# Loading the second attention's first group and the output stage's first operands in earlier stages, in a two-layer transformer kernel on one core

## The chip, the cores and the metric

The kernel runs on one core of one Trainium2 chip. The metric is the device time of one execution in microseconds (us). Three runs of the kernel before gave 3108.98, 3108.89 and 3117.94 us, median 3108.98. A time is told as a difference to that median.

## The reference

The program computes two recurrent layers over x of shape (2, 2048, 256), each of the form `x = x + s * silu(f)` on a layer-normed input. In the first layer `s` is a linear attention and `f` a small transformer block with a mixture of experts. The second layer, with which this change deals, is

```
xn = layernorm(x)
q, k, v = xn @ Wq, xn @ Wk, xn @ Wv            # 16 heads of 32 (real and imaginary halves of 16)
p = softmax(causal(q . k / 4))                 # over 2048 positions
s = concat_heads(p @ v) @ Wo                   # 512 -> 256
f = xn @ quantised_kernel + bias + (xn @ a) @ b
out = x + s * silu(f)
```

All matrix products of the last two stages but the scores are in float32.

## The kernel before, in words

The kernel is a sequence of stages written with hand-placed semaphores. Each stage is a block in which the five engines run their own instruction streams, and a stage ends with a barrier of all engines. The last three stages are these.

**combine_and_project** (tag `p2`) ends the first layer and computes q, k, v and f of the second for eight blocks of 512 rows. Blocks 0 to 3 are the first sequence, 4 to 7 the second. For each block TensorE makes q and k (`L2751`), v (`L2759`) and f (`L2769`), ScalarE writes the upper float16 halves of q and k into `parts` (`L2554`), VectorE the lower halves (`L2651`), and SyncE (SP) stores them in DRAM with four transfers of 512 KB (`L2502`) and v with four of 256 KB (`L2506`). Before ScalarE overwrites `parts` in block b it waits until all stores of block b-1 have landed (`part_out`), and before it overwrites `vt` it waits for the v stores (`v_kept`). SP's queue in a block is: the load of x for block b+2 (`L2485`), the q stores, the k stores, the v stores.

**wide_attention** (tag `at1`) handles 8 groups of 4 heads: groups 0 to 3 are the first sequence. Tiles QT, KT and V of a group are double buffered by `g % 2`, and a group is loaded by six transfers of 512 KB for QT and KT (each of three row bands of 32 holds an upper or a lower half) and one of 1 MB for V, all issued by SP. Work is cut in units (g, u): u is a block of 512 queries. The order of all instructions is fixed beforehand by a small planner, `wide_schedule`, which gives one list `body`; every engine walks that list. Its events are

- S: a score tile in query-major form, only to find row maxima (PE `L990`, VectorE `L932` and `L938`). There are three slots, so S runs at VectorE's pace.
- M, T: the maxima of a unit are turned into a strip of 8 rows of shifts, and SP copies them into rows 96 and 97 of QT with four transfers of 2 KB (`L838`). These are called the strip transfers.
- ST: a score tile in key-major form, with the shifts as two more rows of the contraction (PE `L998`), then the exponential (ScalarE `L912`). The first ST of a unit waits for the unit's strip transfers (`row_ready`).
- PV, SM, A, N, EV: product with V, row sums and output of the unit, which SP stores into `att` (`L824`, 256 KB).

PE runs its instructions in the order of the list, so an S tile that stands behind an ST in the list waits with it. Near the start the list is: 20 S, of which 16 are the unit (0, 0), with M among them, then T of (0, 0), eight S, and the first ST.

In the kernel before, group 0 is loaded at the start of this stage in three portions: columns 0 to 511 of QT by SP and of KT by ScalarE's queue, then the four shift rows of KT, columns 512 to 1023, and a quarter of V. The rest follows behind the strip transfers of unit (0, 0), and group 1 behind those of unit (0, 1). Group g + 2 is loaded when the last unit of group g has ended.

**finish** (tag `fi`) computes `out = x + att @ Wo * g` for 32 tiles of 128 rows. SP loads a 1 MB tile of `att` for each block of 512 rows (`L2793`, `L2799`) and Wo (`L2794`, 512 KB). Each tile is four float32 products of 128 by 256 on PE (`L2841`), a multiplication (`L2824`) and an addition (`L2827`) on VectorE. ScalarE's queue stores blocks of four tiles, 512 KB each (`L2805`). PE, VectorE and ScalarE run hardware loops over blocks.

Of the kernel before, what the change touches and what calls it, by code (L numbers as in the profile page):

```python
# [5 lines left out]
F32 = mybir.dt.float32  # L6
F16 = mybir.dt.float16
# [6 lines left out]
P = 128  # L14
B, T, D, H = 2, 2048, 256, 16
GROUPS = 8
HG = 4
# [705 lines left out]
def wide_attention(nc, tag, C, q_hi, q_lo, k_hi, k_lo, v, out):  # L723
# [17 lines left out]
    with Ctx(nc, tag) as c:  # L741
        QT = [c.sb(f"qT{k}", [P, HG, T], F16) for k in range(2)]
        KT = [c.sb(f"kT{k}", [P, HG, T], F16) for k in range(2)]
        V = [c.sb(f"v{k}", [P, NKC, HG * 32], F32) for k in range(2)]
# [8 lines left out]
        turned = c.sb("turned", [P, QB // 32, 32], F32)  # L753
        column = c.sb("column", [P, QB // 32], F32)
        share = c.sb("share", [P, QB // 32, 32], F32)
# [8 lines left out]
        first_ld = c.sem("first_ld")  # L764
        early_ld = c.sem("early_ld")
        first_v = c.sem("first_v")
        const_ld = [c.sem(f"const_ld{k}") for k in range(2)]
# [23 lines left out]
        def load_qk(eng, g, cols, sem, only=(0, 1)):  # L791
            k = g % 2
            for dst, src, r, which in ((QT, q_hi, 0, 0), (KT, k_hi, 0, 1), (QT, q_lo, 1, 0), (KT, k_hi, 1, 1),
                                       (QT, q_hi, 2, 0), (KT, k_lo, 2, 1)):
                if which not in only:
                    continue
                eng.dma_start(dst[k][r * hd:(r + 1) * hd, :, cols],
                              src[g].rearrange("h d t -> d h t")[:, :, cols]).then_inc(sem, 16)

        def load_v(eng, g):  # L800
            eng.dma_start(V[g % 2][:, :, :], v[g]).then_inc(v_ld[g % 2], 16)

        def load(eng, g):
            load_qk(eng, g, slice(0, T), qk_ld[g % 2])
            load_v(eng, g)

        @block.sync
        def _(sp):
            load_qk(sp, 0, slice(0, QB), first_ld, (0,))
            def shift_rows(k):  # L810
                for h in range(HG):
                    sp.dma_start(KT[k][K:K + 2, h, :], C["shift_rows"][2 * h:2 * h + 2, h, :]
                                 ).then_inc(const_ld[k], 16)

            shift_rows(0)
            load_qk(sp, 0, slice(QB, 2 * QB), early_ld)
            sp.dma_start(V[0][:, 0:4, :], v[0][:, 0:4, :]).then_inc(first_v, 16)
            ended = []

            def store(unit):  # L820
                g, u = unit
                t = place_of[unit]
                sp.wait_ge(scaled, t + 1)
                sp.dma_start(out[g, :, u * QB:(u + 1) * QB], otile[:, t % 2, :]).then_inc(out_stored[t % 2], 16)  # L824

            for ev in body:
# [6 lines left out]
                if ev[0] == "T":  # L833
                    g, u = ev[1]
                    w = place_of[ev[1]]
                    sp.wait_ge(strip_ready, w + 1)
                    for h in range(HG):
                        sp.dma_start(QT[g % 2][K:K + 2, h, u * QB:(u + 1) * QB],  # L838
                                     strip[2 * h:2 * h + 2, w % 2, :]).then_inc(row_ready[w % 2], 16)
                    if w == 0:  # L840
                        sp.dma_start(V[0][:, 4:NKC, :], v[0][:, 4:NKC, :]).then_inc(v_ld[0], 16)
                        load_qk(sp, 0, slice(2 * QB, T), qk_ld[0])
                    elif w == 1:
                        shift_rows(1)
                        load(sp, 1)
                elif ev[0] == "EV" and ev[1] == last_unit[ev[1][0]] and ev[1][0] + 2 < GROUPS:
                    sp.wait_ge(pv_done, quads_done[ev[1]])
                    load(sp, ev[1][0] + 2)
# [36 lines left out]
        def _(act):  # L885
            load_qk(act, 0, slice(0, QB), first_ld, (1,))
# [96 lines left out]
        def _(pe):  # L983
# [22 lines left out]
            pe.wait_ge(C["const_ready"], C["const_count"])  # L1006
            n = pairs = quads = totals = 0
            loaded, valued, first = set(), set(), False
            for ev in body:
                g = ev[1][0]  # L1010
                if ev[0] == "S":
                    if ev[1] == units[0]:
                        if not first:
                            pe.wait_ge(first_ld, QK_LOADS)
                        first = True
                    elif ev[1] == units[1]:
                        pe.wait_ge(early_ld, QK_LOADS)
                    elif g not in loaded:
                        loaded.add(g)
                        pe.wait_ge(qk_ld[g % 2], QK_LOADS * (g // 2 + 1))  # L1020
# [14 lines left out]
                elif ev[0] == "ST":  # L1035
                    _, (g, u), kc, h = ev
                    if kc == 0 and h == 0:
                        if place_of[ev[1]] == 0:
                            pe.wait_ge(const_ld[0], HG * 16)
                        elif g == 1:  # L1040
                            pe.wait_ge(const_ld[1], HG * 16)
# [5 lines left out]
                elif ev[0] == "PV":  # L1047
# [4 lines left out]
                    if ev[1] == units[0]:  # L1052
                        pe.wait_ge(first_v, 16)
                    elif g not in valued:
                        valued.add(g)
                        pe.wait_ge(v_ld[g % 2], 16 * (g // 2 + 1))
# [60 lines left out]


class Steps:

    def __init__(self, sem, names, credit=2):
        self.sem, self.names, self.credit, self.at = sem, list(names), credit, 0
        assert len(set(self.names)) == len(self.names)

    def start(self, eng, blocks_before=None):  # L1130
        eng.nop().then_inc(self.sem, (self.credit if blocks_before is None else blocks_before)
                           * len(self.names))

    def step(self, name, ins):
        assert self.names[self.at] == name, (self.names[self.at], name)
        self.at = (self.at + 1) % len(self.names)
        return ins.then_inc(self.sem, 1)

    def skip(self, eng, names, blk):

        eng.wait_ge(self.sem, (blk + self.credit) * len(self.names) + self.names.index(names[0]))
        for name in names:
            self.step(name, eng.nop())

    def wait(self, eng, name, blk):

        n = len(self.names)
        eng.wait_ge(self.sem, (blk + self.credit) * n + self.names.index(name) + 1)


def blocks(eng, body, per=2):

    with eng.Fori(0, NB // per) as i:
        for k in range(per):
            body(i * per + k, k, i)


def blocks_ahead(eng, body):

    with eng.Fori(0, NB // 2 - 1) as i:  # L1160
        for k in range(2):
            body(i * 2 + k, k, i, False)
    for k in range(2):
        body(NB - 2 + k, k, NB // 2 - 1, k == 1)


class Banks:


    def __init__(self, c, jobs, steps, ring=8):  # L1170
        assert len(jobs) % ring == 0
        self.jobs, self.steps, self.ring = jobs, steps, ring
        self.index = {j[0]: n for n, j in enumerate(jobs)}
        self.banks = [c.ps(f"bank{k}", [P, QB]) for k in range(ring)]

    def bank(self, name):
        return self.banks[self.index[name] % self.ring]

    def take(self, pe, name, blk, *needs):


        n = self.index[name]
        _, eng, drained = self.jobs[n - self.ring]
        last = {}
        for e, step, ago in needs + ((eng, drained, 0 if n >= self.ring else 1),):
            at = (-ago, self.steps[e].names.index(step), step)
            last[e] = max(last.get(e, at), at)
        for e, (ago, _, step) in last.items():
            self.steps[e].wait(pe, step, blk + ago)
        return self.banks[n % self.ring]  # L1190
# [1183 lines left out]
def combine_and_project(nc, C, W, x, exp_out, gather_at, gate, x_all, mix, kvd, w_out, scale_qk, qk_out, v_out,  # L2374
                        w_saved, w_kept):
# [71 lines left out]
    with Ctx(nc, "p2", reuse=True) as c:  # L2447
# [16 lines left out]
        nT = c.sb("nT", [P, 2, 2, NF, P], F32)  # L2464
# [16 lines left out]
        def _(sp):  # L2481
# [292 lines left out]
def finish(nc, W, att, x_all, g_all, out):  # L2774

    jobs = [(f"x{t}", "dve", f"mul{t}") for t in range(4)]
    dve_names = [f"{s}{t}" for t in range(4) for s in ("mul", "add")]
    with Ctx(nc, "fi") as c:
        w = c.sb("w", [P, 4, D], F32)
        a = [c.sb(f"a{k}", [P, 4, QB], F32) for k in range(NB // B)]  # L2780
        o = [c.sb(f"o{k}", [P, 4, D], F32) for k in range(2)]
        w_ld = c.sem("w_ld")
        ld = [c.sem(f"ld{k}") for k in range(NB // B)]
        stored = [c.sem(f"stored{k}") for k in range(2)]
        pe_s = Steps(c.sem("pe"), [j[0] for j in jobs], credit=NB // B)
        dve_s = Steps(c.sem("dve"), dve_names)
        banks = Banks(c, jobs, {"dve": dve_s}, ring=4)
# [161 lines left out]
```

## Time and profile before

| what | us |
|---|---|
| median of three runs | 3108.98 |
| the profiled execution, its own time | 3104.42 |
| span of the profiled execution, first to last instruction | 3102.5 |
| last instruction of the projection (ScalarE, `L2589`) ends | 1971.2 |
| first instruction on PE in the attention | 1978.9 |
| last store of the attention issued | 3030.2 |
| finish, first load issued to the end of the span | 3032.7 to 3102.5 |

All times on the trace are us from the start of the span, durations too unless a unit is given. A name such as SPq is the queue of an engine: the issue of a transfer, not its movement. "to landing" is the time from issue to the moment when all its data is there. A bracket at the end of a row is the time for which the engine was idle before it, and what ended that.

### The profile page before, as it was taken

The page shows a single profiled execution, that of the slowest core. Times are in us where ns is not written, and L with a number is a line of the kernel's source. Part 1 is how long each engine was busy: PE and PEld are TensorE (multiplying, and loading weights), DVE is VectorE, ACT ScalarE, POOL GpSimd, SP SyncE. Part 2 cuts the span into 40 slices and gives each one's busy share as a digit, 9 for nine tenths or more (in the row PEclk, how much of TensorE's full clock was granted, in tenths as well). Part 3 has the DMA queues.
Part 4 walks back from the last instruction along what each step waited for, and adds up shares of the span by engine and source line. Part 5 has one row for each costly group of instructions (what it writes and reads, how often), then busy time and mean ns, then how long its engine had stood idle before and what let it go on. Part 6 is the DMA issues. An engine that isn't in the chain of part 4 may idle for free. (4 is left out here: it accounts for less than half of the span.)

```text
span 3102.5 us, 46462 instructions
## 1 busy us (share of the span) xinstructions
PE 2850.2 (92%) x18025; PEld 1325.8 (43%) x18025; DVE 2022.6 (65%) x4462; ACT 1520.9 (49%) x2473; POOL 929.4 (30%) x420
## 2 busy tenths in 40 slices
PE   7897999999999963999998799799999999999987
PEld 4664233333333341676666555333333333333326
DVE  6886899999999555000001655588887877878823
ACT  3432577677677741222221444245565665565560
POOL 0001000000000022110001320166777777777780
PEclk9998799999999986999999999899999999999998
DMA  3223222022220034222112344421120220211005
GB/s 123 79 61 90 45 42 46 12 45 49 46 46 12 12 112 117 68 72 85 61 48 80 96 149 144 114 62 39 31 62 12 66 62 8 63 35 42 8 10 174
DMA packets 143625, 196.08 MB, mean 63 GB/s; under 512 B 14000, under 2 KB 109056, under 8 KB 141472
## 3 DMA queue, kind: packets, MB, share of 16 engines
q1 hardware_dynamic: 130304, 170.77, 19.8%
q0 software_dynamic: 6144, 16.79, 2.2%
q10 hardware_dynamic: 6960, 5.58, 0.6%
q8 instruction: 141, 2.31, 0.3%
q14 instruction: 76, 0.62, 0.1%
HBM read 116.81 MB, written 75.76 MB: 62 GB/s over the span
## 5 line engine op out<-in xcount | busy, mean ns | idle before, releaser
L912 ACT ACTIVATE at_probs<-at_st 128x512 f32<-128x512 f32 (+3 forms) x1280 | 588.3, 541 | 444.6 <-PE at_st L998 284.1
L874 POOL TENSOR_TENSOR at_probs<-at_probs 128x2048 f32<-128x2048 f32 (+3 forms) x208 | 732.9, 3528 | 220.6 <-ACT at_probs L912 136.8
L383 DVE TENSOR_REDUCE at_part<-at_s 128x1 f32<-128x512 f32 (+3 forms) x1280 | 689.2, 602 | 67.9 <-PE at_s L421 29.8
L365 ACT ACTIVATE at_probs<-at_st 128x1024 f32<-128x1024 f32 (+3 forms) x640 | 541.6, 895 | 275.9 <-PE at_st L440 138.1
L938 DVE TENSOR_REDUCE at_part<-at_s 128x1 f32<-128x512 f32 x768 | 498.4, 683 | 68.6 <-PE at_s L990 64.6
L990 PE MATMUL at_s<-at_kT,at_qT 96*128 96x512 f16 (+3 forms) x1280 | 391.4, 361 | 28.5 <-DMA at_kT<-klo 10.1
L998 PE MATMUL at_st<-at_qT,at_kT 98*128 98x512 f16 (+3 forms) x1280 | 379.3, 356 | 15.1 <-ACT at_probs L912 10.5
L421 PE MATMUL at_s<-at_kT,at_qT 48*128 48x512 f16 (+3 forms) x1280 | 359.6, 366 | 26.4 <-DMA at_qT<-qhi 10.2
L932 DVE CUSTOM_DVE_ANT_0 at_s<-at_s,at_later 128x384 f32<-128x384 f32 (+3 forms) x512 | 246.8, 497 | 109.4 <-PE at_s L990 109.0
L507 PE MATMUL at_acc<-at_probs,at_v 128*32 128x512 f32 (+3 forms) x2560 | 304.5, 549 | 8.9 <-ACT at_otile L352 8.8
L2319 DVE TENSOR_TENSOR ex_ot<-ex_bank,lin_b 128x512 f32<-128x512 f32 x32 | 22.1, 692 | 437.8 <-PE ex_bank L2349 437.8
L1059 PE MATMUL at_acc<-at_probs,at_v 128*32 128x512 f32 (+3 forms) x2560 | 288.3, 538 | 6.7 <-ACT at_otile L894 6.5
L440 PE MATMUL at_st<-at_qT,at_kT 50*128 50x512 f16 (+3 forms) x1280 | 282.4, 356 | 4.9 <-ACT at_probs L365 3.3
L1886 POOL TENSOR_TENSOR ag_a<-ag_a,ag_r 128x1024 f32<-128x1024 f32 x8 | 18.8, 2359 | 849.3 <-ACT ag_r L1903 849.3
L990 PEld LDWEIGHTS at_s<-at_kT,at_qT 96*128 96x128 f16 x1280 | 109.9, 98 | 355.1 <-DVE at_part L938 153.9
L421 PEld LDWEIGHTS at_s<-at_kT,at_qT 48*128 48x128 f16 x1280 | 100.2, 94 | 369.9 <-DVE at_part L383 318.0
L2292 ACT ACTIVATE ex_hT<-ex_bank,ex_b 128x512 f32<-128x512 f32 x128 | 88.0, 687 | 333.2 <-PE ex_bank L2339 333.2
L2339 PE MATMUL ex_bank<-ex_xT,lin_w 128*128 128x512 f32 x512 | 224.0, 595 | 1.0 <-ACT ex_xT L2285 1.0
L2349 PE MATMUL ex_bank<-lin_w,ex_hT 128*128 128x256 f32 x1024 | 223.7, 379 | 0.8 <-ACT ex_hT L2292 0.8
L2349 PEld LDWEIGHTS ex_bank<-lin_w,ex_hT 128*128 128x128 f32 x1024 | 193.9, 190 | 31.1 <-issue 3.8
L998 PEld LDWEIGHTS at_st<-at_qT,at_kT 98*128 98x128 f16 x1280 | 122.9, 98 | 186.1 <-ACT at_probs L912 106.9
L2034 POOL DMA_INDIRECT lin_xin<-z_rows,lin_rows_at x64 | 60.9, 951 | 297.3 <-PE ex_bank L2330 211.4
(322 smaller groups left out, 3229.9 us busy)
## 6 DMA issues: line engine op xcount, KB each, us to landing
att<-at_otile SPq DMA_DIRECT2D x64, 256.0 KB, 2.1
lin_w<-in_W SPq DMA_DIRECT2D x16, 1024.0 KB, 7.7
at_v<-v SPq DMA_DIRECT2D x14, 1024.0 KB, 14.4
v<-pr_vt SPq DMA_DIRECT2D x32, 256.0 KB, 3.2
exp_out<-ex_ot SPq DMA_DIRECT2D x32, 256.0 KB, 2.1
v<-p_vt SPq DMA_DIRECT2D x32, 256.0 KB, 3.7
fi_a<-att SPq DMA_DIRECT2D x8, 1024.0 KB, 6.0
at_qT<-qhi SPq DMA_DIRECT2D x14, 512.0 KB, 9.3
```

The source lines that it names most:

```text
L365: act.activation(probs[:, quad % RING, heads_down * p:heads_down * (p + 1), off:QB], st_ps[n % st_slots][:, :, off:QB], ACT.Exp, scale=EXP ...
L383: dve.tensor_reduce(part[:, w % 2, qt * HG + h, j:j + 1], s_ps[n % S_SLOTS][:, 0:width], AX.X, ALU.max).then_inc(item_free, 1)
L421: mm = pe.matmul(place[:, 0:width], QT[g % 2][rows, h // heads_down, q0:q0 + P], KT[g % 2][rows, h // heads_down, j * QB:j * QB + width], ...
L440: mm = pe.matmul(place[:, y, off:QB], KT[g % 2][rows, h // heads_down, kc * P:(kc + 1) * P], QT[g % 2][rows, h // heads_down, u * QB + off ...
L507: mm = pe.matmul(acc_ps[32 * h:32 * h + 32, off:QB], V[g % 2][:, kc, 32 * h:32 * h + 32], probs[:, quads % RING, h, off:QB], start=kc == 0 ...
L874: pool.tensor_tensor(total, total, probs[:, slots.slot[quad], :, off:QB], ALU.add).then_inc(add_done, 1)
L912: act.activation(probs[:, slots.slot[quad], h, off:QB], st_ps[n % ST_SLOTS][:, off:QB], ACT.Exp, scale=EXP_SCALE).then_inc(exp_done, 1)
L938: dve.tensor_reduce(part[:, w % 2, qt * HG + h, j:j + 1], s_ps[n % S_SLOTS][:, 0:width], AX.X, ALU.max).then_inc(item_free, 1)
L990: pe.matmul(place[:, 0:width], QT[g % 2][0:K, h, q0:q0 + P], KT[g % 2][0:K, h, j * QB:j * QB + width], start=True, stop=True).then_inc(ite ...
L998: mm = pe.matmul(place[:, off:QB], KT[g % 2][0:K + 2, h, kc * P:(kc + 1) * P], QT[g % 2][0:K + 2, h, u * QB + off:(u + 1) * QB], start=Tru ...
L1059: mm = pe.matmul(acc_ps[32 * h:32 * h + 32, off:QB], V[g % 2][:, kc, 32 * h:32 * h + 32], probs[:, slots.slot[quads], h, off:QB], start=kc ...
L2349: mm = pe.matmul(d[:, t * D:(t + 1) * D], hT[cb][:, n, (2 * m + t) * P:(2 * m + t + 1) * P], w2[e % 2][:, n, :], start=n == 0, stop=n == N ...
```

## The change

- An object `Carried` holds one QT, KT and V tile, which live from the projection to the end, and its semaphores. They serve as buffer 0 of the attention. Group 0 is loaded into them whole by SP, in `combine_and_project` at the start of block 4's turn, with 11 transfers (six of 512 KB, four shift rows of 8 KB, V of 1 MB), after a wait for all stores of blocks 0 to 3. The stage's tile `nT` is laid into the V tile.
- At its start the attention has SP load group 1 (six of 512 KB and V of 1 MB) and then its shift rows. PE waits once for group 0. The portioned loads, and those that ScalarE's queue issued, are gone.
- When the last unit of group 6 has ended, SP waits for the stores issued so far, then loads Wo into the V tile and `att` of blocks 0 to 3 into the QT and KT tiles (`load_finish`, 4.5 MB), ahead of the strip transfers of unit (7, 2).
- `finish` starts with these tiles. It is written out without loops, works on pairs of tiles (128 x 512 on VectorE, six PSUM buffers in place of four) and stores 256 KB at a time.

```diff
+class Carried:
+    def __init__(self, c):
+        self.q, self.k = (c.sb(n, [P, HG, T], F16) for n in ("q", "k"))
+        self.v = c.sb("v", [P, NKC, HG * 32], F32)
+        self.group_ld, self.w_ld = c.sem("group_ld"), c.sem("w_ld")
+        self.a_ld = [c.sem(f"a_ld{k}") for k in range(NB // B)]
+        self.w = self.v[:, 0:8, :].rearrange("p (g c) n -> p g (c n)", g=4)
+        self.a = [t[:, 2 * y:2 * y + 2, :].bitcast(F32).rearrange("p a (b n) -> p (a b) n", n=QB)
+                  for t in (self.q, self.k) for y in range(2)]
+    def load_group(self, eng, C, qk, v):
+        K = 32
+        for dst, src, r in ((self.q, qk[0][0], 0), (self.k, qk[1][0], 0), (self.q, qk[0][1], 1),
+                            (self.k, qk[1][0], 1), (self.q, qk[0][0], 2), (self.k, qk[1][1], 2)):
+            eng.dma_start(dst[r * K:(r + 1) * K, :, :], src[0].rearrange("h d t -> d h t")).then_inc(self.group_ld, 16)
+        for h in range(HG):
+            eng.dma_start(self.k[3 * K:3 * K + 2, h, :], C["shift_rows"][2 * h:2 * h + 2, h, :]
+                          ).then_inc(self.group_ld, 16)
+        eng.dma_start(self.v[:, :, :], v[0, 0]).then_inc(self.group_ld, 16)
+    def load_finish(self, eng, W, att):
+        eng.dma_start(self.w, W["Wo"].rearrange("(g p) n -> p g n", p=P)).then_inc(self.w_ld, 16)
+        for blk in range(NB // B):
+            self.load_value(eng, att, blk)
...
 wide_attention, SP
-            load_qk(sp, 0, slice(0, QB), first_ld, (0,))
...
+            load(sp, 1)
+            for h in range(HG):
+                sp.dma_start(KT[1][K:K + 2, h, :], C["shift_rows"][2 * h:2 * h + 2, h, :]).then_inc(const_ld, 16)
...
-                    if w == 0:
-                        sp.dma_start(V[0][:, 4:NKC, :], v[0][:, 4:NKC, :]).then_inc(v_ld[0], 16)
-                        load_qk(sp, 0, slice(2 * QB, T), qk_ld[0])
-                    elif w == 1:
-                        shift_rows(1)
-                        load(sp, 1)
...
+                    elif g + 2 == GROUPS:
+                        sp.wait_ge(pv_done, quads_done[ev[1]])
+                        for k in range(2):
+                            sp.wait_ge(out_stored[k], issued[k])
+                        carried.load_finish(sp, W, out)
...
 wide_attention, PE
+            pe.wait_ge(carried.group_ld, Carried.GROUP_LOADS)
...
 combine_and_project, SP
                 if b + 2 < NB:
                     load_x(b + 2)
+                if b == NQB:
+                    sp.wait_ge(part_out, 64 * NQB)
+                    sp.wait_ge(v_kept, 64 * NQB)
+                    carried.load_group(sp, C, qk_out, v_out)
...
 finish
+            for n in range(PAIRS):
+                tile, rows = o[:, n % 4, :, :], slice(2 * n, 2 * n + 2)
+                if n >= 4:
+                    dve.wait_ge(stored[n % 4], 16 * (n // 4))
+                pe_s.wait(dve, f"x {n}")
+                dve_s.step(f"mul {n}", dve.tensor_tensor(tile, banks.tile(f"x {n}")[:, :, :], g_all[:, rows, :], ALU.mult))
+                dve_s.wait(dve, f"mul {n}")
+                dve_s.step(f"add {n}", dve.tensor_tensor(tile, tile, x_all[:, rows, :], ALU.add))
```

## Rows read from the trace of the kernel before

**Rows 1.** First line of the profile's page.
```profile
span 3102.5 us, 46462 instructions
```
**Rows 2.** Chain that ended last, from 2950 us: start, us, what.
```profile
3032.73 0.37 SPq L2793
...
3033.45 6.48 DMA fi_w<-in_Wo
...
3040.28 57.53 PE fi_bank L2841 x256
...
3098.49 0.43 DVE fi_o L2827
```
**Rows 3.** Line 824 (min/median/max ns, first and last start), and the last output store.
```profile
L824 SPq DMA_DIRECT2D att<-at_otile x32: 320/321/430, 2019.7 to 3030.2; - x32
...
DMA to landing us min/median/max: 2.1/2.1/18.7
...
out<-fi_o ACTq DMA_DIRECT2D x1, 512.0 KB, 2.9
```
**Rows 4.** Stretches of 1 us in finish: us, PE, PEld, DVE, ACT, POOL, clock, DMA share, GB/s.
```profile
3043.00:3044.00 1.00, 1.00 (x4) 0.82 (x3) 0.00 (x0) 0.00 (x0) 0.00 (x0) 0.50 1.06 391
...
3045.00:3046.00 1.00, 1.00 (x6) 0.90 (x5) 0.20 (x1) 0.00 (x0) 0.00 (x0) 1.00 1.04 387
```
**Rows 5.** Timeline of the attention's start: start us, us, engine, line, work, [idle before].
```profile
1972.53 0.33 SPq L797 DMA_DIRECT2D at_qT<-qhi  x1
...
1973.21 0.29 POOL L858 TENSOR_SCALAR_AFFINE_SELECT at_later<-at_later 128x128 bf16<-128x128 bf16 x1
...
1978.95 0.48 PE L990 MATMUL at_s<-at_kT,at_qT 96*128 96x128 f16 x3 [10.08 <-DMA at_kT<-klo]
1979.36 0.30 DVE L932 CUSTOM_DVE_ANT_0 at_s<-at_s,at_later 128x128 f32<-128x128 f32 x1 [6.68 <-PE at_s L990]
...
1989.39 2.45 SPq L838 DMA_DIRECT2D at_qT<-at_strip  x4
...
1993.01 0.59 PE L998 MATMUL at_st<-at_qT,at_kT 98*128 98x512 f16 x1 [0.51 <-DMA at_qT<-at_strip]
```
**Rows 6.** SP's queue at two group loads, and V's time to landing in each.
```profile
2016.18 0.33 SPq L797 DMA_DIRECT2D at_qT<-qhi  x1
...
2019.24 0.43 SPq L801 DMA_DIRECT2D at_v<-v  x1
...
at_v<-v SPq DMA_DIRECT2D x1, 1024.0 KB, 18.5
...
2408.27 0.32 SPq L797 DMA_DIRECT2D at_qT<-qhi  x1
...
2411.91 0.43 SPq L801 DMA_DIRECT2D at_v<-v  x1
...
at_v<-v SPq DMA_DIRECT2D x1, 1024.0 KB, 16.4
```
**Rows 7.** The projection at block 4: SP's queue, two times to landing, ScalarE.
```profile
1868.62 0.87 SPq L2485 DMA_DIRECT2D p_xs<-in_x  x1
1880.56 0.36 SPq L2502 DMA_DIRECT2D qhi<-p_parts  x1
...
1888.82 0.51 SPq L2502 DMA_DIRECT2D klo<-p_parts  x1
...
v<-p_vt SPq DMA_DIRECT2D x1, 256.0 KB, 4.2
...
klo<-p_parts SPq DMA_DIRECT2D x1, 512.0 KB, 4.1
...
1902.52 3.23 ACT L2554 ACTIVATE p_parts<-p_bank,all_score 128x1024 f16<-128x1024 f32 x3
```
**Rows 8.** SP's queue late in the attention: strip transfers of units (7, 2) and (7, 1), (7, 0).
```profile
2917.92 2.40 SPq L838 DMA_DIRECT2D at_qT<-at_strip  x4
...
2959.93 14.04 SPq L838 DMA_DIRECT2D at_qT<-at_strip  x8
```

More of the change, by code:

```diff
@@ L789, in wide_attention, with load @@
         block = c.block()
-        def load_qk(eng, g, cols, sem, only=(0, 1)):
+        def load(eng, g):
             k = g % 2
[L793 to L805, printed above, removed]
+            for dst, src, r in ((QT, q_hi, 0), (KT, k_hi, 0), (QT, q_lo, 1), (KT, k_hi, 1), (QT, q_hi, 2), (KT, k_lo, 2)):
+                eng.dma_start(dst[k][r * hd:(r + 1) * hd, :, :],
+                              src[g].rearrange("h d t -> d h t")).then_inc(qk_ld[k], 16)
+            eng.dma_start(V[k][:, :, :], v[g]).then_inc(v_ld[k], 16)
         @block.sync
         def _(sp):
-            load_qk(sp, 0, slice(0, QB), first_ld, (0,))
[L810 to L818, printed above, removed]
+            load(sp, 1)
+            for h in range(HG):
+                sp.dma_start(KT[1][K:K + 2, h, :], C["shift_rows"][2 * h:2 * h + 2, h, :]).then_inc(const_ld, 16)
+            ended, issued = [], [0, 0]
             def store(unit):
@@ L885, in _ @@
         def _(act):
-            load_qk(act, 0, slice(0, QB), first_ld, (1,))
             n, ended = 0, []
@@ L1116 @@
 EPS = 1e-5
[L1119 to L1190, printed above, removed]
 class Chain:
@@ L2771, in _, with finish @@
                 step(f"y {b}", mm)
-def finish(nc, W, att, x_all, g_all, out):
-    jobs = [(f"x{t}", "dve", f"mul{t}") for t in range(4)]
-    dve_names = [f"{s}{t}" for t in range(4) for s in ("mul", "add")]
+def finish(nc, carried, att, x_all, g_all, out):
+    PAIRS = NT // 2
+    jobs = [(f"x {n}", ("dve", f"mul {n}")) for n in range(PAIRS)]
     with Ctx(nc, "fi") as c:
[L2779 to L2787, printed above, removed]
-        rows = att.rearrange("(b g) r t -> b r g t", b=B)
+        a, w = carried.a, carried.w
+        o = c.sb("o", [P, 4, 2, D], F32)
+        stored = [c.sem(f"stored{k}") for k in range(4)]
+        pe_s = Marks(c.sem("pe"), [j[0] for j in jobs])
+        dve_s = Marks(c.sem("dve"), [f"{s} {n}" for n in range(PAIRS) for s in ("mul", "add")])
+        banks = Banked(c, "bank", [(n, (dve_s, done)) for n, (_, done) in jobs], 6, (P, 2, D))
         block = c.block()
@@ L2801, in _ @@
         @block.scalar
         def _(act):
[L2803 to L2809 removed]
+            rows = out.rearrange("b (n p) d -> p (b n) d", p=P)
+            for n in range(PAIRS):
+                dve_s.wait(act, f"add {n}")
+                act.dma_start(rows[:, 2 * n:2 * n + 2, :], o[:, n % 4, :, :]).then_inc(stored[n % 4], 16)
@@ L2831, in _ @@
         @block.tensor
         def _(pe):
-            pe_s.start(pe)
-            pe.wait_ge(w_ld, 16)
-            def body(blk, k, i):
-                pe.wait_ge(ld[k], i * 16 + 16)
-                for t in range(4):
-                    d = banks.take(pe, f"x{t}", blk)
+            pe.wait_ge(carried.w_ld, 16)
+            for n in range(PAIRS):
+                blk = n // 2
+                k = blk % (NB // B)
+                if n % 2 == 0:
+                    pe.wait_ge(carried.a_ld[k], 16 * (blk // (NB // B) + 1))
+                d = banks.take(pe, f"x {n}")
+                for y in range(2):
+                    t = 2 * (n % 2) + y
```

153 lines of the change are left out of this document (62 added, 91 removed).

## The prediction

> **What bounds the kernel now.** I read the span first [rows 1]: 3102.5 us, against 3104.42 us as the profiled execution's own time, so 1.9 us lie around the trace. The median of the runs shown, 3108.98 us, is 4.6 us above that execution; I work out a difference on the trace and subtract it from the median. The change touches two seams between stages and one stretch in the middle of the projection, so the question at each seam is what ends the idle time there.
>
> At the last seam the chain of waits tells it [rows 2]. SP issues the first load at 3032.73, Wo at 3033.45, Wo is there after 6.48 us, and PE starts at 3040.28. From then on PE alone is the chain, 57.53 us for 32 tiles. Nothing else is on it but the last multiplication, addition and store.
>
> At the seam in front of the attention the timeline tells it [rows 5]. SP's first load goes out at 1972.53, PE had been idle for 10.08 us when it starts at 1978.95, and a transfer ended that. VectorE begins at 1979.36. From there the order is: S tiles at VectorE's pace, the strip transfers issued from 1989.39 to 1991.84, and the first ST at 1993.01, for which PE had waited only 0.51 us. So before, the strip transfers were hardly late.
>
> **Finish: removed wait.** Wo and four blocks of `att` are in place, so PE needs only the barrier. Any instruction behind it can begin when SP's could, at 3032.73; I take 3032.8. That is 3040.28 - 3032.8 = **-7.5 us**, from -7.3 to -7.6. The wait that comes next is the one ahead of it: the last store of the attention, issued at 3030.2 and landed 2.1 us later [rows 3], which the change leaves alone. The first products still run at the low clock: the granted clock is 0.50, the 1.2 GHz level, in the fourth microsecond of PE's work and 1.00 two microseconds later [rows 4]. PE will have been idle for a shorter time before it. Whether its clock is then higher no row shows, so I take nothing for that and put a gain of up to 1.5 us into the bounds, less than the four slow microseconds would give.
>
> **Finish: pairs in place of tiles, no loops.** PE's work is the same. A pair takes PE 57.53 / 16 = 3.6 us. One VectorE instruction on 128 x 256 took 0.43 us [rows 2]; on twice the columns it takes between 0.43 and 0.86, and two of them stay under 1.8 us, hidden behind PE. Only the last pair shows: two instructions longer by about 0.27 each, +0.5 (0 to +0.9). The last store is half as large: 512 KB took 2.9 us to landing and 256 KB took 2.1 on the other queue [rows 3], so -0.8 (-0.8 to 0). Together **-0.3 us**. The loops' own cost doesn't show as a gap on PE; up to -0.5 for it in the range.
>
> **Attention's start: what the engines gain.** PE's first S can start at the barrier, about 1972.6. VectorE's first S needs the mask that GpSimd ends at 1973.21 + 0.29 = 1973.50, so VectorE starts at about 1973.6 instead of 1979.36, 5.8 us earlier. It sets the pace until T, so the strip transfers would be issued from 1983.6 and the first ST start at 1987.2.
>
> **Attention's start: what the queue takes back.** SP now issues 4 MB of group 1 and four shift rows first, from 1972.53, before it comes to the strip transfers. Their issue is over by 1978, so SP itself is free at 1983.6; the question is when the data moves. Two group loads show how long 4 MB take: 2016.18 to 2019.24 + 18.5 = 2037.7, that is 21.6 us, and 2408.27 to 2411.91 + 16.4 = 2428.3, that is 20.0 us [rows 6]. The attention's store issued at 2019.7, right behind the first of these, took 18.7 us to land where the median is 2.1 [rows 3]: it landed at 2038.4, 0.7 us behind V. So a transfer on SP's queue waits for all that was issued before it. By this V of group 1 lands between 1992.5 and 1994.1. The shift rows and strips behind it take some tenths to 1.2 us more (1.2 is what lay between the last strip's issue and the ST before, 1991.84 to 1993.01). The first ST starts at 1993.0 to 1995.3; I take 1994.3. PE meets this ST in its fixed order after eight more S, so from about 1987 on it stands still, and with it VectorE, whose S tiles lie behind the ST. The 5.8 us of lead are lost: from the first ST everything runs as before, but **+1.3 us** late (0 to +2.3). What was moved away (the rest of group 0, group 1) hid behind computing before, and gives nothing.
>
> The Trainium skill, page "DMA: Bandwidth & Descriptors", section "Queues, rings and completion order", says that each DMA engine takes descriptors in ring order but that completion is not in order per issuing engine; the section on why a DMA increments its semaphore by 16 adds that a transfer over two partitions uses only two engines. By that the strips wait for two engines' share and not for the slowest of 16, and the first ST could be 1 or 2 us earlier than 1994.3.
>
> **The projection.** At block 4 SP waits for the v stores of block 3, whose last is issued just before 1868.62 and takes 4.2 us, so until about 1872.3, and issues 11 transfers in 5 us; its next duty is at 1880.56 [rows 7], so the issue is hidden. The x load issued at 1868.62 is ahead in the queue. The 4 MB move until about 1873.5 + 20.6 = 1894.1. The q stores (1880.56) and k stores (until 1888.82) queue behind. 1 MB of them takes at most the 4.1 us of the last one's landing, nearer 3.2 when they stream, so the k stores land at about 1900.9. ScalarE overwrites `parts` at 1902.52. The margin is 1.6 us: **0 us** (0 to +3, if the load or the stores take 4 us more). v and the next x load follow 3 and 5 us later, ahead of their use. If this cover went, PE would stop for want of free banks, one for one.
>
> **Late attention.** `load_finish` stands in front of the strips of unit (7, 2), issued at 2917.92. The 4.5 MB move at the rate of `att` loads, 387 GB/s [rows 4], in 12 us, or at the group loads' rate in 24. The first ST of (7, 2) comes about when the strips of (7, 1) are issued, 2959.93 [rows 8]; there are 42 us of cover, so 0. SP's wait for earlier stores costs at most the 2.1 us of a store's landing, under the same cover.
>
> **The sum**: -7.5 - 0.3 + 1.3 + 0 + 0 = -6.5 us. Against the profiled execution 3104.42 - 6.5 = 3097.9; against the median 3108.98 - 6.5 = **3102.5 us**. A measurement of this kernel can tell about 0.3% (9.3 us) from no change, so this forecast lies within it.
>
> **The rivals.** *The strips are not held back.* Then the start keeps its 5.8 us and the sum is -7.8 - 5.8 = -13.6: 3095.4 us. For it: the strips are 2 KB each, and no row before shows one behind a group load. Against it: the store that took 18.7 us. The Trainium skill's rule above, that completion is not in order per issuing engine, would allow it if the strips' engines ran ahead; ring order on each engine speaks against it. Chance 0.08.
>
> *More is gained than I count.* The mechanism is mine but the strips land 2 us earlier, the clock rises 1.5 us earlier in finish, and the written-out loops give 0.5: -10.5, 3098.5 us. Chance 0.2.
>
> *The projection stalls, and the kernel is slower than before.* Place: ScalarE's wait for block 4's stores ahead of `parts` of block 5. It turns the sign when the k stores land over 1.6 + 6.5 = 8.1 us later than I reckon, after 1909, for instance if the group load took 29 us in place of 20.6 beside a busy PE and VectorE. Each further microsecond costs one, and block 5's x load and v stores are held as well. With a load of 38 us the time is 3112 us, and slower by over 0.3% needs 3118. Against it: the loads of rows 6 ran beside full engines too, and lay between 20.0 and 21.6 us. Chance 0.05 for a loss.
>
> *The change does not do what it says*: group 0 isn't there at the barrier. It is issued 100 us before; no chance of note.
>
> **How the numbers follow.** My forecast has 0.67, the larger gain 0.2, free strips 0.08, a loss 0.05. The forecast's own bounds are 3100 to 3105.5. The range reaches to 3095.5 for the larger gain and most of the free strips, and to 3107.5 for a projection stalled by a few microseconds. Faster by over 0.3% means under 3099.7: all of the free strips, most of the larger gain, and some of the forecast's edge, 0.32. Slower by over 0.3%: 0.03. The rest, 0.65, is within.
>
> **What would show it.** In the profile after: PE's first product in finish directly behind the barrier, some 3 us after the last `att` store; the first S right after 1972.6 and VectorE at 1973.6; the first ST with an idle time of about 7 us ahead, put down to the strip transfer, 21 to 22 us after SP's first load; the projection as long as before; no idle time at the first ST of (7, 2). I am wrong if the first ST starts near 1987, if ScalarE waits in block 5 of the projection, or if the 1040 us between the first ST and the last store change their length by more than 2 us.

## The result, and the profile after

The changed kernel takes **3104.62 us** (median of 20 runs, 3101.92 to 3111.45), the kernel before 3110.87 us in the same session (20 runs, 3106.62 to 3118.58). The ratio is 0.998, with a 95% interval from 0.9973 to 0.9987: 6.2 us less, where 6.5 were forecast.

The profiled execution after took 3104.14 us, its span is the line below. It looks as long as that of before [rows 1], and this is the first trap of the case. The page's first line:

```profile
span 3102.4 us, 46189 instructions
```

The two executions were not equally quick ahead of the change. The x load that SP issues last before block 4's turn stands at 1868.62 us before [rows 7] and at 1874.96 after, though nothing ahead of it was changed. So I count every trace from this load, which is the last common point. From it to the span's end: 3102.5 - 1868.62 = 1233.9 before, 3102.4 - 1874.96 = 1227.4 after, **-6.4 us**, close to the 6.2 of the medians.

SP's queue after, from this load on, in the timeline (start us, us, queue, line, work), with two times to landing and ScalarE's first write over `parts` of block 5, all in order of time but for the two rows of landing times:

```profile
1874.96 0.87 SPq L2417 DMA_DIRECT2D p_xs<-in_x  x1
1878.38 0.33 SPq L737 DMA_DIRECT2D all_q<-qhi  x1
...
1882.67 0.36 SPq L741 DMA_DIRECT2D all_v<-v  x1
1886.91 0.39 SPq L2438 DMA_DIRECT2D qhi<-p_parts  x1
...
1895.19 3.24 SPq L2438 DMA_DIRECT2D klo<-p_parts  x1
1898.47 5.91 SPq L2442 DMA_DIRECT2D v<-p_vt  x4
...
qhi<-p_parts SPq DMA_DIRECT2D x1, 512.0 KB, 14.1
...
klo<-p_parts SPq DMA_DIRECT2D x1, 512.0 KB, 10.5
...
1908.86 1.10 ACT L2490 ACTIVATE p_parts<-p_bank,all_score 128x1024 f16<-128x1024 f32 x1
```

The last k store lands at 1895.19 + 10.5 = 1905.7 and is needed at 1908.86: ScalarE has no wait noted in front. The margin is 3.2 us. New is that SP itself was held: the store of `klo` took 3.24 us to issue, where it took 0.51 [rows 7].

The attention's start after, timeline:

```profile
1978.90 0.34 SPq L822 DMA_DIRECT2D at_qT<-qhi  x1
...
1979.10 0.33 PE L1004 MATMUL at_s<-all_k,all_q 96*128 96x128 f16 x3 [3.89 <-PEq L43]
...
1980.06 0.30 DVE L946 CUSTOM_DVE_ANT_0 at_s<-at_s,at_later 128x128 f32<-128x128 f32 x1 [1.01 <-POOL at_later L873]
...
1981.97 0.44 SPq L824 DMA_DIRECT2D at_v<-v  x1
...
at_v<-v SPq DMA_DIRECT2D x1, 1024.0 KB, 17.6
...
1990.06 2.45 SPq L852 DMA_DIRECT2D all_q<-at_strip  x4
...
2001.16 0.61 PE L1012 MATMUL at_st<-all_q,all_k 98*128 98x512 f16 x1 [8.17 <-DMA all_q<-at_strip]
```

PE starts directly behind the barrier: it stood idle for 3.89 us ahead of its first S instead of 10.08 [rows 5]. But in front of the first ST it now waits 8.17 us, where there were 0.51. V of group 1 lands at 1981.97 + 17.6 = 1999.6.

The chain that ended last, after (start, us, what), and the last store in the timeline:

```profile
3040.23 0.19 issue
3040.42 57.81 PE fi_bank L2760 x256
...
3098.33 0.70 DVE fi_o L2744
...
3099.05 0.69 DVE fi_o L2746
...
3099.78 0.38 ACTq L2733 DMA_DIRECT2D out<-fi_o  x1
```

The 7.55 us from SP's first load to PE [rows 2] are now 0.19 us of issue. Every stretch, against the same one before:

| from, to | before, us | after, us | difference |
|---|---|---|---|
| x load of block 4, SP's first load of the attention | 103.91 | 103.94 | +0.03 |
| that load, first ST | 20.48 | 22.26 | +1.78 |
| first ST, PE's start in finish | 1047.27 | 1039.26 | -8.01 |
| PE in finish | 57.53 | 57.81 | +0.28 |
| PE's end, end of the span | 4.69 | 4.17 | -0.52 |
| sum | 1233.88 | 1227.44 | -6.44 |

### The profile page after: what moved, and what is told of

Same layout as the page of the kernel before. It is cut to its first block and busy times, and to the rows that moved or that the text cites. A ratio compares the mean times of both kernels' runs of the same rounds, so it can differ in the third digit from the quotient of the medians.

```text
span 3102.4 us, 46189 instructions
## 1 busy us (share of the span) xinstructions
PE 2858.1 (92%) x18025; PEld 1329.0 (43%) x18025; DVE 2018.1 (65%) x4430; ACT 1520.7 (49%) x2473; POOL 929.5 (30%) x420
## 5 line engine op out<-in xcount | busy, mean ns | idle before, releaser
L507 PE MATMUL at_acc<-at_probs,at_v 128*32 128x512 f32 (+3 forms) x2560 | 307.2, 554 | 8.9 <-ACT at_otile L352 8.8
L2251 DVE TENSOR_TENSOR ex_ot<-ex_bank,lin_b 128x512 f32<-128x512 f32 x32 | 22.1, 692 | 438.7 <-PE ex_bank L2281 438.7
L1004 PE MATMUL at_s<-all_k,all_q 96*128 96x512 f16 (+3 forms) x640 | 199.5, 367 | 14.6 <-DVE at_part L952 5.6
L1012 PE MATMUL at_st<-all_q,all_k 98*128 98x512 f16 (+3 forms) x640 | 194.8, 362 | 14.4 <-DMA all_q<-at_strip 10.1
L1004 PE MATMUL at_s<-at_kT,at_qT 96*128 96x512 f16 (+3 forms) x640 | 192.3, 356 | 8.2 <-DVE at_part L946 3.8
L1012 PE MATMUL at_st<-at_qT,at_kT 98*128 98x512 f16 (+3 forms) x640 | 185.2, 350 | 8.3 <-ACT at_probs L926 6.6
L2271 PEld LDWEIGHTS ex_bank<-ex_xT,lin_w 128*128 128x128 f32 x512 | 98.1, 192 | 117.8 <-issue 117.0
## 6 DMA issues: line engine op xcount, KB each, us to landing
at_v<-v SPq DMA_DIRECT2D x11, 1024.0 KB, 11.1
```

The costliest lines, as they stand in the source:

```text
L507: mm = pe.matmul(acc_ps[32 * h:32 * h + 32, off:QB], V[g % 2][:, kc, 32 * h:32 * h + 32], probs[:, quads % RING, h, off:QB], start=kc == 0 ...
L1004: pe.matmul(place[:, 0:width], QT[g % 2][0:K, h, q0:q0 + P], KT[g % 2][0:K, h, j * QB:j * QB + width], start=True, stop=True).then_inc(ite ...
L1012: mm = pe.matmul(place[:, off:QB], KT[g % 2][0:K + 2, h, kc * P:(kc + 1) * P], QT[g % 2][0:K + 2, h, u * QB + off:(u + 1) * QB], start=Tru ...
L2271: mm = pe.matmul(d[:, :], w1[e % 2][:, n, f * P:(f + 1) * P], xT[:, n, cb * QB:(cb + 1) * QB], start=n == 0, stop=n == NF - 1)
```

## The experiments

**The theory under test** was that of the forecast: finish gives 7.5 us, and the attention's start gives nothing, because the strip transfers stand behind 4 MB of group 1 on SP's queue. Its rivals are that it is not the order in one queue, since small transfers are slow on whatever queue they are issued while 4 MB are moving; and that the early loads don't matter, since computing sets the pace of the start.

The changed kernel again, with nothing edited, as the base of what follows:

> The changed kernel once more, unaltered, as the mark for the runs beside it. Expected 6 us below the kernel before. In the first trace of it everything ahead of the change (up to the x load of the projection's block 4, line 2417) ended 6.3 us later than in the trace of the kernel before. My theory: that is a difference between executions, so this trace may put the point anywhere from 1868 to 1876, while the stretch from there to the end stays at 1227.4 us within 1 us. Rival: the change of memory layout made the earlier stages slower, then the point stands at 1875 again and the kernel before has it near 1868.6 in each run.

Measured: 3103.62 us (12 runs, 3101.49 to 3112.26) against 3111.01 (25 runs), ratio 0.9976 (0.9966 to 0.9986). Its trace is 1227.8 us from the common point to the end. First ST, out of the timeline:

```profile
2002.49 0.61 PE L1012 MATMUL at_st<-all_q,all_k 98*128 98x512 f16 x1 [8.11 <-DMA all_q<-at_strip]
```

The wait of 8.1 us repeats. From SP's first load to this ST are 22.21 us.

**Group 1 later.** SP loads group 1 and its shift rows behind the strip transfers of unit (0, 1), as the kernel before did.

```diff
-            load(sp, 1)
-            for h in range(HG): ... shift rows of KT[1]
...
+                    if w == 1:
+                        load(sp, 1)
+                        for h in range(HG): ... shift rows of KT[1]
```

> One part undone: group 1 is loaded behind the strip transfers of unit (0, 1), as in the kernel before, not at the attention's start. Theory (strips wait in SP's queue behind 4 MB): strips issued at the same time as before, 11.2 us after SP's first instruction of the stage, and the first ST 1.2 us behind their last issue, so 14.8 us after PE's first S and not 22.3; no idle time over 1 us ahead of it; 7.5 us faster than the changed kernel, 13.5 us faster than the kernel before. Rival (what is gained there is lost again, since 4 MB now stand in front of the store and the strips of units (0, 0) and (0, 2)): gain under 3 us. No gain at all would mean that the first ST waited for something else.

Measured: 3095.93 us (5 runs, 3094.58 to 3096.59), ratio 0.995 (0.9938 to 0.9963): 7.7 us under the changed kernel and 15.1 under the one before. Timeline of its start:

```profile
1976.06 0.48 PE L1006 MATMUL at_s<-all_k,all_q 96*128 96x128 f16 x3 [3.88 <-PEq L43]
...
1987.04 2.46 SPq L849 DMA_DIRECT2D all_q<-at_strip  x4
...
1990.57 0.61 PE L1014 MATMUL at_st<-all_q,all_k 98*128 98x512 f16 x1 [0.61 <-DMA all_q<-at_strip]
```

The first ST comes 14.51 us after the first S, where it came 22.02 us after it in the changed kernel (1980.47 to 2002.49). The wait has gone and 7.5 us with it, so computing does not set the pace of the start. In the trace the stretch between the first ST and PE's start in finish is 1.5 us longer (1041.07 us against 1039.59), and PE in finish takes 0.5 longer (58.38 against 57.89): from the common point to the end this trace is 1222.3 us, 5.6 less than the 1227.8 above. The runs say 7.7; I take the saving as 6 to 8 us. No step has to have lost the 1.5 us: from the first ST to the barrier of finish the two traces of the kernel before (the second is at the end of this section) have 1039.65 and 1040.75, and two of kernels that start it as changed have 1039.07 and 1040.47; here it is 1040.88.

**Group 1 early, strips on ScalarE's queue.** It leaves the 4 MB where the change put them and takes only unit (0, 0)'s strips off SP.

```diff
-                    for h in range(HG):
+                    for h in range(HG) if w else ():
...
+            act.wait_ge(strip_ready, 1)
+            for h in range(HG):
+                act.dma_start(QT[0][K:K + 2, h, 0:QB], strip[2 * h:2 * h + 2, 0, :]).then_inc(row_ready[0], 16)
```

> Group 1 is still loaded first, but the four strip transfers of unit (0, 0) are issued by ScalarE on its own queue. Theory (what holds the strips is the order within one queue): they land within 2 to 3 us of their issue although 4 MB are moving, the first ST starts about 15 us after the first S, 7 us faster than the changed kernel. Rival (the strips wait because all 16 engines are full, whatever the queue): the first ST stays at about 22 us after the first S and the time at that of the changed kernel.

Measured: 3102.48 us (7 runs), ratio 0.9971 (0.996 to 0.9982), only 1.1 us less than the changed kernel. ScalarE's queue and PE in the timeline, with V's time to landing (issued at 1982.81):

```profile
1990.95 2.98 ACTq L903 DMA_DIRECT2D all_q<-at_strip  x4
...
2000.84 0.61 PE L1015 MATMUL at_st<-all_q,all_k 98*128 98x512 f16 x1 [6.96 <-DMA all_q<-at_strip]
...
at_v<-v SPq DMA_DIRECT2D x1, 1024.0 KB, 17.9
```

Nothing stands ahead of the strips on their own queue, and they still need 6.9 us from the end of their issue (1993.93) to the ST; V lands at 2000.7. The theory, as far as it rests on the order in one queue alone, falls here. Either a queue beside a full one is served in turn with it, but slowly, or the strips wait for all that is outstanding on every queue. Here both give 2001, since V lands then.

**8 MB ahead of the strips** tells them apart: SP issues four copies of 1 MB from `v` to a spare tensor in memory behind group 1, first with the strips on SP, then with the strips on ScalarE.

```diff
             load(sp, 1)
+            for n in range(4):
+                sp.dma_start(spare[n], v[n]).then_inc(spared, 16)
```

> The suspected cost doubled: at the attention's start SP issues, between group 1 and its shift rows, four more copies of 1 MB each from v to an unused DRAM tensor, so that 8 MB stand before the strip transfers of unit (0, 0) on SP's queue. Theory (queue order): the first ST waits until all of it has moved, 12 to 22 us longer than in r1, that is 34 to 44 us after the first S. Rival (the strips have a latency of some 8 us beside any bulk transfer, whatever is in front): first ST 22 us after the first S, as in r1.

> The same 8 MB on SP's queue, but the four strip transfers are issued by ScalarE, as in r3. In r3 they did not escape: the first ST came 20.9 us after the first S, just when V of group 1 had landed. Theory A (another queue is served in turn with the full one, in large portions on the two engines that a strip uses): the strips take 6 to 9 us from their issue however much is queued, so the first ST is again 19 to 23 us after the first S. Theory B (a small transfer on another queue still completes only when the engines have finished what was issued before it): the first ST comes as late as in r5, 34 to 44 us.

Measured, one execution each: 3115.18 and 3106.36 us, beside 3108.21 of the kernel before. First ST with the strips on SP (first fence, first S at 1977.65) and on ScalarE (second, first S at 1977.93):

```profile
2009.93 0.61 PE L1017 MATMUL at_st<-all_q,all_k 98*128 98x512 f16 x1 [18.38 <-DMA all_q<-at_strip]
```

```profile
1988.91 2.98 ACTq L908 DMA_DIRECT2D all_q<-at_strip  x4
...
2000.81 0.61 PE L1020 MATMUL at_st<-all_q,all_k 98*128 98x512 f16 x1 [8.99 <-DMA all_q<-at_strip]
...
spare<-v SPq DMA_DIRECT2D x4, 23.2
```

On SP's queue the copies put the first ST from 22.0 to 32.3 us after the first S, less than the 34 that I had as the least, but the theory's way: the copies take 20.0 to 26.5 us to landing there, the last one is issued at 1982.9 and so lands at about 2009.4, and the ST follows 0.5 us later. On ScalarE's queue the ST comes after 22.9 us, at 2000.81. The copies (first issued at 1981.3, last at 1983.1, 19.7 to 26.6 us to landing) are through only at about 2009.7, 9 us later. But V of group 1, issued first as before, had landed at 1980.81 + 17.4 = 1998.2.

**The copies first, then group 1**, strips on ScalarE: now 4 MB more stand ahead of group 1, too.

> As r6 (8 MB on SP's queue, strips of unit (0, 0) on ScalarE's), but the four copies to the unused DRAM tensor are issued ahead of group 1. In r6 the first ST came 22.9 us after the first S, 2.7 us behind the landing of V and some 7 us before the last copy was done, so it may have waited for group 1 and not for a turn. Here V of group 1 lands about 9 us later, near 30 us after the first S. Theory A (the other queue is served in turn): the strips still land 7 to 9 us after their issue, first ST 20 to 23 us after the first S. Theory C (strips on whichever queue complete only when the loads into SBUF issued before them are done): 29 to 33 us.

Measured: 3122.94 us, on another chip, where the kernel before takes 3133.04 (3128.78 to 3136.81), so that only stretches within the trace are compared. ScalarE's queue and PE in the timeline, then the share of time for which the DMA engines were busy, in tenths, and what they moved, in slices of 1.125 us from 1985 to 2030:

```profile
2007.14 2.98 ACTq L908 DMA_DIRECT2D all_q<-at_strip  x4
...
2018.21 0.61 PE L1020 MATMUL at_st<-all_q,all_k 98*128 98x512 f16 x1 [8.15 <-DMA all_q<-at_strip]
...
DMA  6990089930590960919922799999999999998930
GB/s 235 340 345 13 0 238 285 290 120 0 175 757 0 699 233 0 881 58 350 524 58 44 127 299 189 198 202 198 206 197 211 233 200 208 197 240 291 430 109 0
```

The ST comes 22.1 us after the first S (1996.15). The bursts of up to 881 GB/s, 4.2 MB together, are the copies; they are over by 2009. Then group 1 moves at some 200 GB/s until about 2028, 10 us behind the ST. The strips on ScalarE's queue needed 6.9, 8.9 and 8.1 us from the end of their issue in the three runs. So waiting for everything outstanding is excluded: in the last run the end of group 1, in the one before all copies land behind the ST. What is left is this: on SP's queue the strips wait for what was issued before them; on another queue they do not, but eight rows of 1 KB still take 7 to 9 us beside the bulk transfers, against 1.1 when nothing else moves (1987.04 + 2.46 to 1990.57 with group 1 later). The Trainium skill, page "DMA: Bandwidth & Descriptors", section "Queues, rings and completion order", says that each DMA engine goes round between the queues it has work for, a packet at a time. The last two of these runs agree that a second queue is not behind the first; that the 6 to 8 us are what such turns cost is my reading, which no run shows by itself.

**Finish without early loads.** `load_finish` moves from the end of group 6 to the start of finish's SP; all else is as changed.

```diff
-                        carried.load_finish(sp, W, out)
...
+            carried.load_finish(sp, W_all, att)
```

> One part undone: Wo and the four blocks of att are loaded at the start of the output stage by SP, not during the attention; the stage is still written out in pairs. Theory (the gain of the last seam is the load's latency): PE's first product 6 to 7.5 us behind SP's first issue, 6.5 to 7.5 us slower than the changed kernel, that is about 0 to 1 us slower than the kernel before. From PE's first product to the end of the span the same as in the changed kernel within 0.5 us. Rival (the 4.5 MB during group 7 cost something, or the gain came from the written-out pairs): under 5 us slower.

Measured: 3109.59 us (11 runs, 3108.63 to 3112.18), ratio 0.9999 (0.9991 to 1.0008), 6.0 us over the changed kernel. The chain of waits, from the barrier on (SP's first load of the stage goes out at 3039.54):

```profile
3039.98 6.27 DMA all_q<-att
...
3046.38 57.28 PE fi_bank L2760 x256
...
3103.75 0.70 DVE fi_o L2744
```

The wait is back: PE starts 6.84 us behind SP's first load, and from the barrier (3039.48) to the end of the span the stage takes 68.3 us, where the changed kernel has 62.2 (3040.23 to 3102.4). These 6.15 us are the 6.0 of the runs, a little less than the 6.5 to 7.5 that I had expected, since PE's tiles take 57.28 us here against 57.81. The kernel is back at the time of the one before, whose stage took 69.8 us: the written-out finish still gains some 1.5 us, and the attention's start loses about as much.

**Finish alone.** The other way round, on a slower chip, on which the changed kernel itself was not run: the attention's start and the projection of the kernel before, with the new finish and its early loads.

> One part alone: the output stage as changed (operands loaded during group 7, written out in pairs), while the attention starts as in the kernel before, with group 0 loaded at its start in portions and group 1 behind unit (0, 1). Theory (the early load of group 0 with group 1 at the start gives nothing as it stands): first ST about 20.9 us after SP's first instruction of the stage in place of 22.3, 7 to 8 us faster than the kernel before, that is the same as the changed kernel or up to 2 us faster. Rival (the changed start gains): this kernel is more than 2 us slower than the changed kernel.

Measured: 3123.76 us (7 runs, 3118.81 to 3127.54) against 3133.04, ratio 0.9972 (0.9961 to 0.9983). The changed kernel has 0.998 and 0.9976. By the ratios the finish alone gives all that the change gives. Its first ST and its last chain:

```profile
2014.73 0.58 PE L1035 MATMUL at_st<-all_q,all_k 98*128 98x512 f16 x1 [0.50 <-DMA all_q<-at_strip]
...
3054.94 57.95 PE fi_bank L2787 x256
```

SP's first load is at 1993.97 there, so the first ST comes 20.76 us behind it, as before the change (20.48, and 20.94 in the second trace) and sooner than after it (22.26, and 22.04 to 22.33 in three more traces with this start). That is the early group 0 with group 1 at the start: a loss of 1.1 to 1.8 us.

**Group 0 behind block 4's q stores.** SP issues the first two stores of block 4 ahead of `load_group`, and k and v behind it. That takes away the margin in front of `parts`.

```diff
-                if b == NQB: ... carried.load_group(sp, C, qk_out, v_out)
...
+                    if b == NQB and side == 0:
+                        sp.wait_ge(v_kept, 64 * NQB)
+                        carried.load_group(sp, C, qk_out, v_out)
```

> Group 0 is loaded in the projection behind the q stores of block 4, 8 us later than in the changed kernel. This moves 4 MB directly in front of the k stores on whose landing ScalarE waits before block 5. By queue order: load from about 13 us after the x load's issue, over at 34, then the k stores, landed at about 37 to 38 us after it; ScalarE needs them 33.9 us after it (2522 in the first traces: 1868.62 to 1902.52). Theory: ScalarE waits 3 to 5 us there, PE's banks fill, and the kernel is 3 to 5 us slower than the changed kernel (3106.5 to 3108.5 where r1 has 3103.6). Rival (the stores are not on a path, or overtake): the same time as r1 within 1.5 us.

Measured: 3111.33 us (10 runs, 3108.78 to 3118.16), ratio 1.0013 (1.0003 to 1.0023), so about 11 us over the changed kernel by the two ratios, where I had expected 3 to 5. In its trace the stretch from the x load of block 4 (1870.97) to SP's first load of the attention (1982.07) is 111.1 us instead of 103.9. SP, ScalarE and PE in the timeline, and the granted clock in the stretches behind (us, PE, PEld, DVE, ACT, POOL, clock, DMA share, GB/s):

```profile
1893.41 14.76 SPq L2441 DMA_DIRECT2D v<-p_vt  x4
1908.21 1.41 SPq L2417 DMA_DIRECT2D p_xs<-in_x  x1
...
1909.62 1.11 ACT L2489 ACTIVATE p_parts<-p_bank,all_score 128x1024 f16<-128x1024 f32 x1 [4.66 <-DMA klo<-p_parts]
...
1912.10 6.12 PE L2686 MATMUL p_bank<-p_xT,p_w 128*128 128x512 f32 x8 [5.15 <-DVE p_parts L2586]
```

```profile
1908.00:1910.00 2.00, 0.00 (x0) 0.00 (x0) 0.00 (x0) 0.39 (x1) 0.00 (x0) 1.00 1.13 352
...
1912.00:1914.00 2.00, 1.90 (x3) 0.87 (x4) 2.00 (x3) 0.74 (x1) 0.00 (x0) 0.50 0.58 179
...
1918.00:1920.00 2.00, 2.00 (x6) 0.95 (x5) 1.61 (x9) 1.72 (x2) 0.00 (x0) 1.00 0.00 0
```

The named place of the rival "the projection stalls" is real: ScalarE waits 4.66 us for the `klo` store, and PE stands 5.15 us behind it. Then comes a cost that I hadn't counted: the granted clock was 1.00 while PE worked and still in the first part of its stop, PE restarts at 0.50, the 1.2 GHz level, and these eight products take 6.12 us instead of 3.70 (the same line before, at 1904.99). 4.7 and 2.4 are 7.1, the 7.2 us that the stretch grew by. From the common point to the end the trace is 1236.0 us, 8.2 to 8.6 over the two of the changed kernel. The intervals of the two ratios leave some 7 to 15 us, so the 11 are not at odds with the trace; what may be lost beyond it no trace here shows.

**The kernel before, once more**, to see how far two traces of one kernel differ ahead of the change.

> The kernel before, unaltered, for a second trace of it. In its first trace the x load of the projection's block 4 (line 2485, the last but one) was issued at 1868.6, in four traces of changed kernels 4 to 8 us later, although nothing ahead of that point was changed in what is computed. Theory (differences between executions, and the first trace was a quick one: 3104.4 us against a median of 3111): the point lies between 1872 and 1878 this time, and the stretch from there to the end is again 1233.9 us within 1.5. Rival (the new layout costs the earlier stages some us): 1868.6 again.

Measured: 3111.03 us. The common point stands at 1873.89, where the first trace had it at 1868.62 and the changed kernels, the slower chip left out, have it between 1870.97 and 1876.36; from it to the span's end are 1235.4 us (1233.9 in the first). So the 6.3 us by which the first trace of before was ahead come from the execution: the same kernel is 5.3 us later here; and two traces of the same kernel differ by 1.5 us behind that point, which is what a single pair of traces can tell here.

## Why the prediction was right

**The sum** was -6.5 us; the runs have -6.2 and the traces -6.4. By its terms:

- **Finish, the removed wait: -7.5.** Right. PE follows the barrier after 0.19 us instead of 7.62 (3032.66 to 3040.28), 7.4 us less. Undoing the early loads alone brings back 6.0 us in the runs. The whole stage is 7.7 us shorter, so that part of what I put down to the wait belongs to writing the stage out: with late loads it is 1.5 us shorter, where I had 0.3 for that. What was left open, an earlier rise of the clock after a shorter idle time, did not come: PE's first four microseconds still have a granted clock of 0.50, and the fifth has 0.66, where it had 0.96 before. PE's 32 tiles take 0.28 us longer with it; over all traces PE takes 57.8 to 58.4 us with early loads and 57.3 to 57.7 with late ones.
- **Pairs and half stores: -0.3.** Right: two instructions of 0.69 us (I had 0.43 to 0.86), and 0.52 us less from PE's end to the end of the span. Together with PE's 0.28 that makes -0.24.
- **What the engines gain at the attention's start.** VectorE starts 1.16 us behind SP's first load, where I had 1.07, and the strip transfers are issued 11.16 us behind it, where I had 11.1.
- **What the queue takes back: +1.3.** The size was right (+1.78 in the trace, 1.1 to 1.8 over all of them; ST 22.26 us behind SP's first load instead of 21.8), and V landed 20.7 us behind it, inside the 20.0 to 21.6. The 1 or 2 us by which the ST might have been earlier than that did not show. The step behind it holds for the queue that the kernel uses: a transfer on SP's queue waits for all that was issued before it, as the run with 8 MB shows, where the first ST comes 10.3 us later. It was only half of the matter. The order in the queue is not the only cost: on an empty second queue the strips are 1.1 us sooner and no more, so 4 MB in flight cost nearly as much there. That the two come to the same time within 1.5 us is chance, a matter of how large this load is and when the strips are issued; with 8 MB they are 9.4 us apart. The same step had me expect 7 us from the other queue in that run, and it gave 1.1.
- **The projection: 0.** Right, and with 3.2 us of margin instead of 1.6: the k stores landed at 1895.19 + 10.5 = 1905.7, earlier than I had them (1900.9, and 6.3 more for the later common point, gives 1907.2).
- **Late attention: 0.** Right. No idle time for the strips of (7, 2), and the stretch from the first ST to the barrier is 0.6 us shorter, inside the 2 us I had allowed.

**The rivals.** "The strips are not held back" fell for the changed kernel, and it gives its time once the group load is moved away: I had priced it at 13.6 us less than before, and that edit measured 15.1 less in the runs and 11.6 to 13.1 in the traces. The stalled projection was no matter of chance here but of order: with two stores ahead of the load instead of none it comes, and then it costs not one for one, as I had written, but about one and a half (4.7 us of wait made 7.2), since the clock falls too. That clause failed.

**Slips beside the sum.** By my own sum a group load of 38 us gives 3118 us, not the 3112 that I wrote: it is 17.4 us over the 20.6, the first 8.1 bring the kernel back to its time before, and 9.3 are left. 3112 would need some 31.5 us. And I held 9.3 us for the least that can be told from no change: over 20 runs of each kernel the interval is 4.0 to 8.4 us less, so the gain is clear of none, though smaller than that.

## What to carry to other kernels

A load that is hoisted to the start of a stage is not free because its engine is idle: a small transfer behind it on its queue waits for all of it (some 20 us for 4 MB), and on the other queue tried here it still took 7 to 9 us, so put the bulk load behind the first small transfer on which computing waits. Here that one move, with the rest of the change kept, turned -6 us into **-15 us** by the medians (3095.93, the best of all versions run, faster than both kernels), and into -12 to -13 by the traces. And when two traces are laid side by side, start counting from the last instruction that the change could not touch.

## What the runs showed of the hardware that was not expected

- **A second queue is no fast lane beside a full one.** Eight rows of 1 KB need 6.9, 8.9 and 8.1 us from the end of their issue while loads or copies issued on SP's queue are still moving, and 1.1 us without.
- **The issuing engine is held up, too.** With the group load, the q stores and k stores outstanding, a store that takes SP 0.51 us to issue took 3.24, and the four v stores 5.91 us; with the group load between the q and the k stores these four took 14.76. With the copies issued ahead of group 1 the four shift rows took 4.49 us to issue instead of 1.19, but only 1.33 with the copies behind group 1, though as many bytes had been issued by then. So it is not the bytes alone, and what it goes by no run shows. A plan of SP's time that adds up issue costs from a quiet stretch is too short by this.
- **A stop of PE costs more than its length.** 5.15 us of idle time, at whose start the granted clock was 1.00, were followed by eight products that began at the 1.2 GHz level and took 2.4 us more than before.
